# Two states of lead for the rows of B in the mixer's transfer queue

## The reference

```
dt, Bc, Cc = jnp.split(x_dbl, [DT_RANK, DT_RANK + D_STATE], axis=-1)
dA  = jnp.exp(dt[..., None] * A)                        # A = -exp(A_log)
dBx = dt[..., None] * Bc[:, :, None, :] * xc[..., None]
h   = dA_t * h + dBx_t                                  # over time, for 512 channels and 16 states
y   = jnp.einsum('bdn,bn->bd', h, C_t)
y   = (ys + Dp * xc) * silu(z)
```

## Time and profile before

| | us |
|---|---|
| median of three timed runs | 6441.31 |
| the profiled execution | 6432.63 |
| its span | 6430.8 |
| PE busy | 5521.3 (86%) |
| VectorE busy | 4731.1 (74%) |
| ScalarE busy | 4438.4 (69%) |
| GpSimd busy | 3904.5 (61%) |
| time in matmul weight loads (beside PE) | 3587.8 (56%) |

### The profile page before, as it was taken

How to read it: one execution, slowest core, us unless ns; L and a number is a source line. 1 busy time by engine, 2 the same in 40 slices (tenths; PEclk the granted TensorE clock), 3 DMA queues, 4 the chain that set the end, 5 groups by cost and what they waited for, 6 DMA issues and landing times. The chain is left out here.

```text
span 6430.8 us, 126264 instructions
## 1 busy us (share of the span) xinstructions
PE 5521.3 (86%) x40354; PEld 3587.8 (56%) x40354; DVE 4731.1 (74%) x6028; ACT 4438.4 (69%) x7115; POOL 3904.5 (61%) x2143
## 2 busy tenths in 40 slices
PE   3688888888888888888688868998989979999999
PEld 3466666666566665665444435554555546666665
DVE  1688888888888888888799949999999971221221
ACT  1698999989899888999746658888888851111111
POOL 2677777777777777777434439999999960000000
PEclk7899999999999999999989979999999999999999
DMA  1212121121212112120144555555555541111110
GB/s 34 43 28 46 28 43 32 26 45 28 46 28 42 32 27 45 27 46 16 31 143 175 208 183 193 205 186 186 192 191 195 202 159 47 33 33 49 33 33 10
DMA packets 470057, 538.16 MB, mean 84 GB/s; under 512 B 251056, under 2 KB 345008, under 8 KB 469568
## 3 DMA queue, kind: packets, MB, share of 16 engines
q1 hardware_dynamic: 469568, 531.63, 27.0%
HBM read 370.18 MB, written 161.35 MB: 83 GB/s over the span
## 5 line engine op out<-in xcount | busy, mean ns | idle before, releaser
L317 DVE CUSTOM_DVE_ANT_0 srow<-srow,ps_s,cur 128x1024 f32<-128x1024 f32 x1024 | 1303.4, 1273 | 259.5 <-PE ps_s L465 179.5
L394 ACT ACTIVATE srow<-srow,nmax 128x1024 f32<-128x1024 f32 x1024 | 1191.1, 1163 | 204.7 <-DVE nmax L317 192.4
L403 ACT COPY AT<-ps_t 128x512 f32<-128x512 f32 x2048 | 1104.7, 597 | 70.3 <-PE ps_t L476 69.3
L476 PEld LDWEIGHTS ps_t<-ident,srow 128*128 128x128 f32 x8192 | 961.7, 143 | 279.1 <-ACT AT L403 84.8
L476 PE MATMUL ps_t<-ident,srow 128*128 128x128 f32 x8192 | 1102.9, 278 | 13.2 <-ACT AT L403 8.8
L1724 POOL TENSOR_TENSOR c_hc<-c_hs,c_cs 128x1024 f32<-128x1024 f32 x432 | 1010.5, 2374 | 27.9 <-DVE c_hs L1825 25.6
L465 PE MATMUL ps_s<-K,Q 96*128 96x512 bf16 x2048 | 631.2, 390 | 436.4 <-DVE nmax L317 320.5
L306 DVE SCALAR_TENSOR_TENSOR srow<-ps_p,rho,R 128x1024 f32<-128x1024 f32 x768 | 975.0, 1270 | 13.7 <-ACT ps_p L357 9.2
L1685 PE MATMUL c_ps_y<-c_hc,c_ident 128*128 128x512 f32 x2048 | 957.6, 601 | 1.5
L1825 DVE TENSOR_TENSOR_SCAN c_hs<-c_da,c_pd 128x1024 f32<-128x1024 f32 x384 | 864.5, 2275 | 53.1 <-PE c_pd L1676 51.5
L1769 ACT ACTIVATE c_sT<-c_dxT,c_bT 128x256 f32<-128x256 f32 x1536 | 668.4, 494 | 142.9 <-PE c_pd L1676 133.5
(11 more groups left out here) (196 smaller groups left out, 8631.9 us busy)
## 6 DMA issues: line engine op xcount, KB each, us to landing
c_cs<-bc_d SPq DMA_DIRECT2D x256, 512.0 KB, 4.1
c_bs<-bc_d SPq DMA_DIRECT2D x64, 512.0 KB, 4.7
parts_d<-parts SPq DMA_DIRECT2D x65, 384.0 KB, 3.3
K<-parts_d SPq DMA_DIRECT2D x192, 128.0 KB, 4.5
Q<-parts_d SPq DMA_DIRECT2D x384, 64.0 KB, 2.9
sz_d<-b_sz SPq DMA_DIRECT2D x16, 1024.0 KB, 8.1
xv_d<-b_xv SPq DMA_DIRECT2D x16, 1024.0 KB, 5.6
dt_d<-b_ab SPq DMA_DIRECT2D x16, 1024.0 KB, 5.4
```

The source lines that it names most:

```text
L317: nc.vector.tensor_tensor_reduce(r[:], r[:], ps_s[:], cur[k][:, h:h + 1], BIG, ALU.add, ALU.min, nmax[:, h % NROW:h % NROW + 1]).then_inc( ...
L394: nc.scalar.activation(r[:], r[:], ACT.Exp, scale=-1.0, bias=nmax[:, h % NROW:h % NROW + 1]).then_inc(e_ok, 1)
L403: nc.scalar.copy(AT[h % NAT][:, HG * half:HG * half + HG, :], ps_t[:, half]).then_inc(at_ok, 1)
L476: last = nc.tensor.transpose(ps_t[:, half, i, :], rows_sb[h % NROW][:, j * P:(j + 1) * P], ident[:])
```

## The change

In SyncE's order the row of B is asked for two states earlier, and ahead of the row of C of that state where it was behind it: row 5 at n = 1 (before, at the end of n = 3, behind the loads), row 9 at n = 5 (7), row 13 at n = 9 (11), and row 1 of the next pair at n = 13 (15). The waits in `spread_b`, the buffers and the orders of all other engines are the same.

```diff
             def body(q, b, p, first, last):
                 next_b = b + p
                 for n in range(NS):
+                    if n + 4 in ROWS_N and n > 0:
+                        spread_b(q, b, n + 4)
+                    if n + 4 == NS + ROWS_N[0] and not last:
+                        spread_b(q + 1, next_b, ROWS_N[0])
                     spread_c(q, b, n)
                     if n == 3 and not last:
                         alone(sp, da_ok, at(q, UNITS, (NS - 1, 1), -1), sp_own)
...
                         if not first:
                             store(q - 1, b - 1 + p, 1 - p)
                             load_end(q, b, p)
-                    if n + 2 in ROWS_N and n > 0:
-                        spread_b(q, b, n + 2)
-                    if n == NS - 1 and not last:
-                        spread_b(q + 1, next_b, ROWS_N[0])
```

## The result

| us | before | after |
|---|---|---|
| timed median (lowest to highest, 4 runs each) | 6440.24 (6436.87 to 6442.36) | 6501.74 (6497.91 to 6502.83) |
| span of the profiled execution | 6430.8 | 6496.1 |

The ratio of after to before is 1.0093, with a 95% interval of 1.0080 to 1.0105: slower by 0.9%, clear of the noise. Forecast was 6500.

A forecast was written before the change was run, and what follows sets the result against it. Taken to bind: the order of work between VectorE and GpSimd, not a busy sum. Pairs 1 to 14 at 91.78 against 87.54 us, +59 us, take the median 6441.3 to 6500 us; own range 6488 to 6512, 8 in 10: 6437 to 6512.

The forecast's parts named there:

- The stall goes in 14 pairs: In pairs 1 to 14, B's row 5 lands some 20 us before use, ending waits of 76.2 us, 5.4 us each.
- The other three rows cost nothing: B's rows 9, 13 and next pair's 1, ahead of C rows: taken as nothing, at most 4.7 us a pair.
- The cover of up to 22 us: A C row is asked for four states of 5.5 us ahead, so a delay by a B row is hidden.
- The first gating is shut out until GpSimd runs dry: At state 5 in pairs 1 to 14, VectorE's gating multiplication takes 8.00 us as in pair 15, plus 0.29 us.
- The stretches behind: After state 5's second scan: 37.63 us to state 13, then 34.71 us to the next gating; 91.78 us a pair altogether.
- The total: +4.24 us a pair times 14, +59 us, bringing the timed median to 6500 us, +0.9%; chance 66%.
- The range's own upper end, 6512: Own range 6488 to 6512, from 0.4 us a pair less and 5.5 us of timed-run span on either side.
- Rival 1: VectorE's gating gets in at the next end of a GpSimd instruction: 84.6 us a pair, -41 us, 6400; chance 20%.
- Rivals 2 and 3: Gatings wait one further GpSimd instruction, 6464, chance 9%; or row 5 still late or a C row waits, about 6441, 5%.

The follow-up runs named there:

- all_but_row5: Changed kernel with B's row 5 asked for behind the four loads again, rows 9, 13 and 1 still early: 6447.9 us, 1.0007 of the kernel before.
- gating_from_psum: Changed kernel with the skip term written back to PSUM and the gating multiplication reading it there, one SBUF input: 6400.3 us, 0.9941 of the kernel before.
- own_wait_before_b5: Changed kernel with GpSimd waiting for its own last C product before state 5's first product: 6401.8 us in a single execution.
- only_row5: Kernel before with only B's row 5 asked for early, ahead of C's row 1: 6499.1 us, 1.0093 of the kernel before.
- own_waits_both: Changed kernel with GpSimd waiting for its own last instruction before state 5's first product and before state 3's first C product: 6406.1 us, 0.9942 of the kernel before.

## Why the prediction was right, point by point

- **The stall goes in 14 pairs.** Right: only the first wait for a B row is left, 23.4 us. In pair 4 row 5 goes out 16.6 us ahead of the loads and lands 21.2 us before its use (some 17 and 20 in the forecast).
- **The other three rows cost nothing.** Right for the changed kernel, and all_but_row5 can't be told from before in time. With row 5 late the wait for C's row 9 is real, 10.8 us in the stage. The cover of up to 22 us, from four states of lead, was too large: in pair 4 of the changed kernel the row is asked for 13.8 us before its use, since the buffer is released by GpSimd, which lags, and it takes 9.0 us to land. So this term was nothing with 4.7 us to spare.
- **The first gating is shut out until GpSimd runs dry.** Right: 8.17 to 8.32 us in pairs 1 to 14, where the sum had 8.00 + 0.29, and 19.15 + 0.29 us to state 5's second scan. In pair 4 that is 4265.00 - 4245.56 = 19.44.
- **The stretches behind.** 4302.57 - 4265.00 = 37.57 and 4337.27 - 4302.57 = 34.70 us, where 37.63 and 34.71 stood in the sum. A pair: 91.75 against 91.78.
- **The total.** 14 x 4.21 = 58.9 us in the stage (59 forecast), 61.5 between the medians; the rest is within what runs differ by. The range's own upper end, 6512, does not follow from the two terms named for it, which give 6505.5; the result lies below both.
- **Rival 1** (VectorE gets in at the next end): false here, but real elsewhere. Its premise holds after short runs of GpSimd, and its time, 6400, is what gating_from_psum and own_wait_before_b5 reach (6400.3, 6401.8). I had set at least six gapless instructions against it, and the identical place in pair 15. Only the second was a safe reason: with five VectorE still gets in each time, and the actual number in pairs 1 to 14, twenty, was not read from the trace. The forecast is a copy of what pair 15 showed once; it did not know why VectorE is shut out.
- **Rivals 2 and 3**: neither a gating of 3.7 us nor a late row 5 was seen in the changed kernel.

The Trainium skill (SBUF — State Buffer, "Who interferes with whom") names the pair of conditions, two SBUF inputs on VectorE and reads by GpSimd, and gating_from_psum agrees: 8.3 us becomes 1.22 us with one SBUF input. The rule that the prediction read to the letter, that whoever starts first holds the shared ports for its whole instruction, is worded in that section for VectorE's two-port modes, and the prediction took it over to this multiplication. It does not tell what these runs show: VectorE waited through three further instructions of GpSimd.

## What to carry to other kernels

A stall of one engine can be the only opening that another one has: here GpSimd's wait for row 5 was where VectorE's gating got in. Before a wait of GpSimd is removed, look at what VectorE runs beside it, and above all for VectorE instructions with both inputs in SBUF. A single long instruction in a line that is otherwise short, in the one place where the stall is already missing, tells what the removal will cost. Two cures worked here: to read one input from PSUM, or to let GpSimd wait once for its own last instruction just ahead of the contested place.

## What the runs showed of the hardware

- A VectorE multiplication with two SBUF inputs (1.19 us alone) waited through up to three gapless GpSimd multiplications after the one that was running, 8.0 to 8.3 us in all in 28 of the 30 cases of after and only_row5 (7.6 and 7.9 in the two with two further ones). Whether it is let in between two of them went with how many instructions GpSimd had run without a gap: 1 and 5, always (15 of 15 each); 11, 5 of 15; 20, never (30 cases).
- A wait of GpSimd for its own last instruction, one per pair, left a gap of 0.37 to 0.51 us in own_wait_before_b5. The changed kernel took 6501.7 us without it and 6401.8 us with it, in a single execution; own_waits_both, with two such waits, took 6406.1 us in four.
- The wait shows in no list of waits: it is inside the duration of the instruction and counts as busy time, 144.1 us for 32 instructions that need 39 (32 x 1.22).
